# Routing tokens to experts in another order, and the first attention's keys ahead of its second queries

## The reference: what is computed

```python
x = x + L0_xattn(layernorm(x), ctx, mask, Wq, Wk, Wv, Wo)   # 16 query heads, 8 kv heads
x = x + L0_ffn(layernorm(x), ...)                           # width 1536, weights rounded to fp8
x = x + L1_xattn(layernorm(x), ctx, ..., gq, gk)            # q and k RMS-normalised
x = x + L1_ffn(layernorm(x), gate_w, gate_up, down)         # 16 experts, best 2 of each token

# routing, in L1_ffn
p = sigmoid(x @ gate_w.T)
p = p / sum(p)
w, idx = top_k(p, 2)
w = w / sum(w)
```

## Time and profile of the kernel before

| | us |
|---|---|
| median of 3 runs (lowest to highest) | 2182.91 (2182.68 to 2184.34) |
| the profiled execution, device time | 2181.82 |
| its span in the trace | 2180.0 |
| busy in the span: PE / DVE / ACT / POOL | 2073.1 / 1565.5 / 1258.0 / 504.5 |
| mean granted TensorE clock | 0.984 of 2.4 GHz |

### The profile page before, as it was taken

The page is one execution under the profiler, slowest core; times in us unless marked ns, Lnnn a source line. Parts: engine busy times, 40 slices in busy tenths (PEclk is TensorE's granted clock), DMA queues, the critical chain, the costliest instruction groups (busy, mean ns, idle before and its releaser), DMA issues. The chain is left out here.

```text
span 2180.0 us, 33659 instructions
## 1 busy us (share of the span) xinstructions
PE 2073.1 (95%) x11642; PEld 1788.1 (82%) x11642; DVE 1565.5 (72%) x3690; ACT 1258.0 (58%) x3249; POOL 504.5 (23%) x622
## 2 busy tenths in 40 slices
PE   7999999999999999999999999999999999599992
PEld 6888888988888778887888888888888887378882
DVE  6777687677779984434777777777777778767775
ACT  5555454445455534324776676777666666567771
POOL 2001011001000002223233333323332322145441
PEclk9999999999999999999999999999999999799996
DMA  7231222122221220002111111111221111288876
GB/s 256 78 124 67 73 81 90 59 90 69 85 74 39 80 71 1 1 0 78 49 62 65 58 49 59 49 58 49 71 72 53 49 40 39 87 279 291 292 270 258
DMA packets 78536, 202.51 MB, mean 93 GB/s; under 512 B 8688, under 2 KB 38408, under 8 KB 66208
## 3 DMA queue, kind: packets, MB, share of 16 engines
q1 hardware_dynamic: 68672, 179.37, 23.5%
q0 software_dynamic: 7520, 16.80, 2.3%
q10 hardware_dynamic: 2176, 4.19, 0.5%
HBM read 179.09 MB, written 29.10 MB: 95 GB/s over the span
## 5 line engine op out<-in xcount | busy, mean ns | idle before, releaser
L1319 DVE TENSOR_TENSOR l_pT_lo<-bank,l_pT_hi 128x512 fp32r<-128x512 f32 x256 | 175.4, 685 | 70.6 <-ACT l_pT_hi L1123 70.6
L1117 ACT ACTIVATE l_probs<-l_scored,l_nbias 128x256 f32<-128x256 f32 x256 | 128.6, 505 | 165.8 <-DVE l_nbias L1392 165.8
L755 PE MATMUL bank<-l_wkv_hi,l_ctxT 128*128 128x512 f32 (+1 forms) x768 | 221.1, 359 | 1.5 <-PEq L92 0.6
L755 PE MATMUL bank<-xnT_hi,l_wq_hi 128*128 128x512 f32 x512 | 209.0, 408 | 1.4 <-DVEq L1665 0.7
L755 PE MATMUL bank<-l_wo_hi,l_oT_hi 128*128 128x512 f32 x512 | 209.1, 408 | 0.7 <-DVE l_oT_lo L1319 0.7
L755 PE MATMUL bank<-l_wo_hi,l_oT_lo 128*128 128x512 f32 x512 | 200.6, 392 | 0.0
L755 PE MATMUL bank<-xnT_hi,l_wq_lo 128*128 128x512 f32 x512 | 200.2, 391 | 0.0
L755 PE MATMUL bank<-xnT_lo,l_wq_hi 128*128 128x512 f32 x512 | 199.9, 390 | 0.0
L755 PE MATMUL bank<-l_wo_lo,l_oT_hi 128*128 128x512 f32 x512 | 199.8, 390 | 0.0
L1407 DVE TENSOR_SCALAR l_probs<-l_probs,l_rden 128x256 f32<-128x256 f32 x512 | 187.8, 409 | 9.0
L1123 ACT CAST l_pT_hi<-bank 128x512 fp32r<-128x512 f32 x256 | 150.7, 589 | 62.4 <-PE bank L854 58.4
(11 more groups left out here) (299 smaller groups left out, 5736.5 us busy)
## 6 DMA issues: line engine op xcount, KB each, us to landing
l_ctxT<-ctx_split SPq DMA_DIRECT2D x63, 1024.0 KB, 4.8
moe_raw_gu<-in_L_ffn_gate_up_proj SPq DMA_DIRECT2D x31, 1024.0 KB, 6.4
moe_raw_dn<-in_L_ffn_down_proj SPq DMA_DIRECT2D x31, 512.0 KB, 5.5
l_raw_a<-in_L_xattn_Wq SPq DMA_DIRECT2D x16, 512.0 KB, 5.8
l_raw_a<-in_L_xattn_Wo SPq DMA_DIRECT2D x16, 512.0 KB, 5.8
x_sb<-in_x SPq DMA_DIRECT2D x4, 1024.0 KB, 8.2
l_v_next<-l_kn SPq DMA_DIRECT2D x16, 256.0 KB, 2.0
l_v_lo<-l_v_next SPq DMA_DIRECT2D x16, 256.0 KB, 2.6
```

What stands on the lines that cost most here:

```text
L755: mm = nc.tensor.matmul(out, a[x], b[y], start=(i == 0), stop=(i == n - 1))
L1117: ins = nc.scalar.activation(probs[u % 2][:, t, :], src, ACT.Exp, bias=nbias[:, i:i + 1], scale=scale, accum_out=rsum[:, i:i + 1])
L1319: nc.vector.tensor_tensor(pair[1], src, pair[0].bitcast(F32), ALU.subtract).then_inc(done, 1)
```

## The change

It moves and removes instructions at the two places.

First attention: on DVE the mask bias goes ahead of both query splits, and the key split ahead of the second query split; the first `biases` goes ahead of the turned rows' low parts. On ACT the key copy goes ahead of the normalisations (now three rows together) and of the second query copy. On PE the first scores go ahead of all four row transposes.

Routing: ACT normalises tiles 8 to 11 and takes the sigmoids of groups 0 and 1 in the second attention's block, with the table load at `gate_high`; PE transposes group 0's sigmoids there. In the experts block ACT, POOL and DVE normalise tiles 14, 15 and 12 to 13; there are two `probT` tiles, five turn banks, one copy out of PSUM for two groups. The division by the sum moves from `best_two` (3 instructions in each call) to behind the list of rows (4 instructions). The two multiply and sum steps ahead of the halves become one pair of double width.

```diff
@@ first attention @@
             pe.sem_inc(y_made, TG)
-            if AHEAD:
-                turn_rows(0, 1)
             scores(0, 0, 0)
             if AHEAD:
-                turn_rows(2, 3)
+                turn_rows(0, 1, 2, 3)
...
+                copy_q(*PROLOGUE, 0)
+                copy_k(*PROLOGUE, 0)
+                normalise(0, 1, 2)
+                copy_q(*PROLOGUE, 1)
             if AHEAD:
-                normalise(2, 3)
+                normalise(3)
                 act.wait_ge(k.ctx_stored, 16 * NG)
                 turned_high(0, 1)
             exponentials(0, 0, 0)
...
                 first_moments()
+                dve.wait_ge(const_in, 16)
+                nc.vector.tensor_scalar(mask_bias[:, :], mask_u8[:, :], -MASKED, MASKED, ALU.mult, ALU.add).then_inc(dve_chain, 1)
+                dve.wait_ge(dve_chain, 1)
...
                 split_q(*PROLOGUE, 0)
-                split_q(*PROLOGUE, 1)
-                dve.wait_ge(const_in, 16)
-                nc.vector.tensor_scalar(mask_bias[:, :], mask_u8[:, :], -MASKED, MASKED, ALU.mult, ALU.add).then_inc(dve_chain, 1)
-                dve.wait_ge(dve_chain, 1)
             dve.sem_inc(o_split, 1)
             for h in range(nkv):
                 split_k(*PROLOGUE, h)
+            split_q(*PROLOGUE, 1)
...
+            biases(0, 0, 0)
             if AHEAD:
                 turned_low(0, 1)
-            biases(0, 0, 0)
@@ end of the second attention, PE then ACT @@
                     following.logits(pe, g)
+                following.turn_probs(pe, 0)
...
                 following.gate_high(act)
+                act.wait_ge(ln_factors, LATE // TG + 2)
+                following.normalise(act, LATE)
+                following.sigmoids(act, 0)
+                for t in range(LATE + 1, LATE + TG):
+                    following.normalise(act, t)
+                following.sigmoids(act, 1)
@@ experts block, POOL, PE, ACT @@
+            gp.tensor_scalar(xn[:, POOL_TILE, :], k.x_sb[:, POOL_TILE, :], rstd[:, POOL_TILE:POOL_TILE + 1], shift[:, POOL_TILE:POOL_TILE + 1],
+                             ALU.mult, ALU.add).then_inc(pool_normed, 1)
...
-            for t in range(LATE, LATE + TG):
-                turn(t)
-            turn_probs(0)
-            for t in range(LATE + TG, NT):
-                turn(t)
-            turn_probs(1)
+            start.turn_probs(pe, 1)
+            for t in range(LATE, NT):
+                turn(t)
...
             for t in range(LATE, LATE + TG):
                 turned_high(t)
-            nc.scalar.activation(warm[:, 0:1], k.ident[:, 0:1], ACT.Sigmoid)
-            sigmoids(0)
-            turned_high(LATE + TG)
             copy_probs(0)
-            sigmoids(1)
-            turned_high(LATE + TG + 1)
-            copy_probs(1)
-            for t in range(LATE + TG + 2, NT):
+            for t in range(LATE + TG, NT):
                 turned_high(t)
             for g in (2, 3):
-                sigmoids(g)
-                copy_probs(g)
+                start.sigmoids(act, g)
+            copy_probs(1)
@@ experts block, DVE @@
-                chain(v.tensor_reduce(ms[:, at], prob[:, at, :], AX.X, ALU.add))
-                chain(v.reciprocal(ms[:, at], ms[:, at]))
-                chain(v.tensor_tensor(prob[:, at, :], prob[:, at, :], each(ms[:, at], E), ALU.mult))
...
+            chain(v.tensor_tensor(hsel[:, :, :, :].rearrange("p c t e -> p c (t e)"), pick[:, :, :, :].rearrange("p c t e -> p c (t e)"),
+                                  per(place[:, :, :].rearrange("p t e -> p (t e)"), 2), ALU.mult))
+            chain(v.tensor_reduce(half[:, :, :], hsel[:, :, :, :], AX.X, ALU.add))
             for c in range(2):
-                chain(v.tensor_tensor(hsel[:, c, :, :], pick[:, c, :, :], place[:, :, :], ALU.mult))
-                chain(v.tensor_reduce(half[:, c, :], hsel[:, c, :, :], AX.X, ALU.add))
...
+            chain(v.tensor_reduce(ms[:, :], prob[:, :, :], AX.X, ALU.add))
+            chain(v.reciprocal(ms[:, :], ms[:, :]))
+            chain(v.tensor_tensor(m1[:, :], m1[:, :], ms[:, :], ALU.mult))
+            chain(v.tensor_tensor(m2[:, :], m2[:, :], ms[:, :], ALU.mult))
```

More of the change, by code:

```diff
@@ L2151, in logits, with normalise, sigmoids, turn_probs @@
         mm.then_inc(a.logits_made, 1)
+    def normalise(act, t):
+        nc.scalar.activation(a.xn[:, t, :], k.x_sb[:, t, :], ACT.Identity, bias=k.ln_shift[:, t:t + 1],
+                             scale=k.ln_rstd[:, t:t + 1]).then_inc(a.early_normed, 1)
+    def sigmoids(act, g):
+        act.wait_ge(a.logits_made, g + 1)
+        if g >= 2:
+            act.wait_ge(a.probs_turned, g - 1)
+        nc.scalar.activation(a.probT[g % 2][:, :], a.b_logits[g % 2][0:E, :], ACT.Sigmoid).then_inc(a.sigmoids_made, 1)
+    def turn_probs(pe, g):
+        pe.wait_ge(a.sigmoids_made, g + 1)
+        for t in range(TG):
+            at = TG * g + t
+            mm = nc.tensor.transpose(a.b_probs[:, E * at:E * (at + 1)], a.probT[g % 2][:, P * t:P * (t + 1)], k.ident[0:E, 0:E])
+        mm.then_inc(a.probs_turned, 1)
     a.turn_gate, a.gate_high, a.gate_low, a.logits = turn_gate, gate_high, gate_low, logits
+    a.normalise, a.sigmoids, a.turn_probs = normalise, sigmoids, turn_probs
     a.sync = lambda sp: sp.dma_start(a.gw[:, :], gate_w).then_inc(a.gw_in, 16)
@@ L2172, in moe_stage @@
     BY_PAIR, BY_HALF = (1.5 * 2.0 ** 23 * n for n in (2 * P, P))
-    DVE_TILES = tuple(range(LATE + TG, NT))
-    ACT_TILES = [t for t in range(LATE, NT) if t not in DVE_TILES]
+    DVE_TILES, ACT_TILE, POOL_TILE = (LATE + TG, LATE + TG + 1), LATE + TG + 2, LATE + TG + 3
     y_rows = nc.dram_tensor("moe_y_rows", (2 * T, D), F32, kind="Internal").ap()
@@ L2195, in moe_stage @@
         assert nc.sbuf_base == w_at + 4 * (4 * GU + 4 * DN)
-        xn = at_place("xn", w_at, [P, NT, D], F32)
+        xn = start.xn
+        assert w_at == start.xn_at
         dn_at = w_at + 4 * 4 * GU
@@ L2420, in _ @@
             for g in (2, 3):
-                turn_probs(g)
+                start.turn_probs(pe, g)
             pe.wait_ge(consts_made, 14)
@@ L2503, in _ @@
         def _(act):
-            def normalise(t):
-                nc.scalar.activation(xn[:, t, :], k.x_sb[:, t, :], ACT.Identity, bias=shift[:, t:t + 1], scale=rstd[:, t:t + 1]).then_inc(act_normed, 1)
             def turned_high(t):
                 act.wait_ge(turned, t - LATE + 1)
-                nc.scalar.copy(k.xnT_hi[:, :, P * t:P * (t + 1)], b_turn[t % len(b_turn)][:, :].rearrange("p (k t) -> p k t", k=KD)).then_inc(turned_hi, 1)
-            def sigmoids(g):
-                act.wait_ge(logits_made, g + 1)
-                due(act, probs_turned, g)
-                nc.scalar.activation(probT[:, :], b_logits[g % 2][0:E, :], ACT.Sigmoid).then_inc(sigmoids_made, 1)
@@ L2516, in copy_probs @@
-            def copy_probs(g):
-                act.wait_ge(probs_turned, g + 1)
-                nc.scalar.copy(prob[:, of_group(g), :].rearrange("p t e -> p (t e)"), b_probs[:, 0:TG * E]).then_inc(probs_copied, 1)
-            for t in ACT_TILES:
-                normalise(t)
+                nc.scalar.copy(k.xnT_hi[:, :, P * t:P * (t + 1)], turn_bank(t)[:, :].rearrange("p (k t) -> p k t", k=KD)).then_inc(turned_hi, 1)
+            def copy_probs(i):
+                at = slice(*PARTS[i])
+                act.wait_ge(probs_turned, 2 * (i + 1))
+                nc.scalar.copy(prob[:, at, :].rearrange("p t e -> p (t e)"), b_probs[:, E * at.start:E * at.stop]).then_inc(probs_copied, 1)
@@ L2522, in _ @@
+            nc.scalar.activation(xn[:, ACT_TILE, :], k.x_sb[:, ACT_TILE, :], ACT.Identity, bias=shift[:, ACT_TILE:ACT_TILE + 1],
+                                 scale=rstd[:, ACT_TILE:ACT_TILE + 1]).then_inc(start.early_normed, 1)
             for t in range(LATE, LATE + TG):
                 turned_high(t)
-            nc.scalar.activation(warm[:, 0:1], k.ident[:, 0:1], ACT.Sigmoid)
-            sigmoids(0)
-            turned_high(LATE + TG)
             copy_probs(0)
-            sigmoids(1)
```

84 lines of the change are left out of this document (42 added, 42 removed).

## The result

| | before | after |
|---|---|---|
| median, us (lowest to highest) | 2183.19 (2182.68 to 2184.34, 4 runs) | 2169.29 (2169.04 to 2169.92, 4 runs) |
| the profiled execution, device time | 2181.82 | 2169.92 |
| its span | 2180.0 | 2167.8 |

I had forecast 2173.3 us, in a range of 2170.3 to 2177.3. The sign and the largest term were right; the size was not. The times in this document are of one state of the core; a single execution of before_filler ran in another (2995.85 us at a mean granted clock of 0.652) and is left out of its ratio.

A forecast was written before the change was run, and what follows sets the result against it. TensorE's waits at the first attention and in routing's chain were taken as what can be gained: 2.0 - 0.2 + 7.65 + 0.05 + 0.4 - 0.3 = 9.6, so 2182.9 - 9.6 = 2173.3 us, range 2170.3 to 2177.3.

The forecast's parts named there:

- the step on the four new instructions: Behind the list: some 1.2 us of DVE work delays the expert weights' low parts, covered by over 2 us in hand.
- First attention: Start of the kernel: earlier key copy and mask work bring scores to 38.8 and turned probabilities to 46.05, gain 2.0.
- the hold of POOL: First attention: DVE's mask work over POOL's power costs POOL all of DVE's 1.2 us, so factors come at 37.85.
- The unstretched walk: First attention without POOL losing time to the mask work: turning at 45.0, gain 3.0 in place of 2.0.
- rival (a): Mask work doesn't stretch POOL's power, and TensorE keeps 2.4 GHz through the ranking: gains 3.0 and 0.5, 2171.8 us; chance 0.22.
- Block start: Second attention's tail: with ACT last, the experts block begins at 1859.85 in place of 1859.65, cost 0.2.
- Routing: Experts block: second logits from 1864.4, not 1870.50, and the choice ends at 1875.3, not 1882.95, gain 7.65.
- (b): Routing: TensorE's clock falls during the turns, 2.5 to 4 us lost, 2176.5 us; chance 0.15.
- (c): Routing is moved but not shortened, gathered rows wait for something not moved: 2180.5 us; chance 0.03.
- (d): Clock falls before the turns and returns only behind the filling matmuls: 11.5 lost against 9.6, 2184.8 us; chance 0.02.
- Merged step: Ahead of the halves: two multiply and sum steps of double width take 1.45 us where four took 1.83, gain 0.4.
- Filling matmuls: Ahead of the expert loop: nothing can be gained, and a later return of the clock loses 0.3.

The follow-up runs named there:

- before_filler: The kernel before with four more DVE instructions, writing a tile nobody reads, ahead of the first expert weights' low parts; 2180.72 us against 2182.42, ratio 0.9992.
- before_load_waits: The kernel before with SP's second gate and up load waiting for the second gather's landing; 2180.97 us against 2182.07, ratio 0.9996.
- after_again: The changed kernel run once more, unchanged, beside the kernel before on the same chip; 2169.14 us, ratio 0.9939.
- divide_first: The changed kernel with the division by the probabilities' sum also ahead of the choice again, three instructions for each half of the tokens; 2170.32 us.
- keep16: The changed kernel with 16 filling matmuls ahead of the experts in place of 24; 2168.39 us.
- tail_undone: The changed kernel with ACT's normalising of tiles 8 to 11, the first two sigmoids and TensorE's first turn back in the experts block; 2173.7 us.

## Why the prediction was wrong

**What failed: the step on the four new instructions.** It said that they stand behind the list, delay the first expert weights' low parts, that over 2 us are in hand, and so cost nothing. The cover was there, and the cost was nothing. But I asked only who needs the low parts, and not what the low parts release. They free the buffer that SP's next load waits for; SP's issue moved from 0.9 us ahead of the third gather to 0.7 behind it, and the gathers landed early. First to fourth turning took 1.63 us less, forecast 0. before_filler and before_load_waits show it. The loop from the first filling matmul to the end, which I had put at 277 us as before, took 276.2 (277.4 before). Rows 7 had the filling matmuls and the first turning, but no gather, no load, and not the second to fourth turning: the prediction carried the loop over as a block of 277 us, though its opening isn't steady.

**First attention: the mechanism was right, its size wrong.** Scores at 38.8: 38.76. The term was the hold of POOL: from rows 4, where a DVE instruction of 0.54 us lay inside a power that took 0.49 more, I read that POOL loses all of DVE's time, and took 1.2 us. That step failed: the row's power ended 0.05 us behind DVE's instruction, and in the four traces of the table where the power loses time it is its end that is held. In rows 4 another of DVE's one-input instructions, 1043.52 to 1044.06, lies over the power's start, so that place alone could be read in more than one way. My own estimate of the landing, 34.4, would then have given DVE's end at 35.7, ahead of the power's own end at 35.97, and a loss of 0. Measured were 0.77 (after, where the mask had landed by 33.70 and POOL's small first instruction was held), 0 (after_again) and at most 0.42. The unstretched walk gave turning at 45.0, and it came at 44.95 in after_again and at 44.95 to 45.29 in six of the eight traces with the early mask: this part of rival (a) fits better than my forecast. Its other part, the full clock through the ranking, didn't come (0.54 in 1870 to 1896). The rule of the Trainium skill ("SBUF — State Buffer", section "SBUF: two separate sides") that I had weighed there, that the second to come is blocked for a whole instruction, fits none of the table's rows: the second was DVE, and it took its 1.23 us in each.

**Block start: 0 for 0.2.** ACT's last sigmoids end at 1856.87 and POOL's factors at 1856.70; the distance from the first logits to the block start is 6.63 us in both kernels, so by these two traces ACT's tail had just room; what sets the distance isn't shown. The sum also held this cost twice: the walk through the experts block starts at 1859.95, so its end of the choice at 1875.3, and with it the 7.65, already had the later start in it. Without that slip the forecast would have been 2173.1.

**Routing: right.** 4.17 us to the second logits (forecast 4.5), 15.15 to the end of the choice (15.4), in all 8.13 for 7.7. Clock at 1.00 through the turns, as the forecast needed; rivals (b), (c) and (d) are out. Of the missing 0.4, some 0.2 are the start counted twice; the rest is that turns took 3.97 us and no more, and DVE's low parts ran without gaps. **Merged step: right**, 0.37 for 0.4; **division: right**, 0.91 for 0.9 by divide_first.

**Filling matmuls: -0.68 for -0.3.** The granted clock came back 4.3 us after the first filling matmul (2.4 before), and the matmuls took 7.74 us. In the other traces with 24 of them it came back after 1.7 to 4.7 us, and they took 6.51 to 7.91. The prediction said that nothing can be gained at this place; in keep16 the fourth turning came 1.35 us sooner after the first filling matmul than in after. Before, the rows landed just as the filling ended; in the changed kernel they land sooner, and the filling is a loss.

**The range.** I gave unknown costs, all on one side: what might be lost at the filling matmuls, what POOL might lose. For an earlier opening of the loop there was no term and no rival, so the range ended at 2170.3. With 1.6 for the opening and rival (a)'s first attention (3.0), the same sum would have given some 2170.7 us. The rest (about 1.4) is the distance of single executions from their medians, the start counted twice and small gains in three places; it isn't taken apart further.

## What to carry to other kernels

When an instruction is put in "where there is room", follow what the delayed instructions release, not only who consumes their results: a freed buffer starts a transfer, and the order of transfers decides what lands in time. A large load that isn't needed soon should be issued behind the small gathers that are; one wait on the loading queue gave the shorter opening here, without any detour over an engine. And where filling work meets data that lands at the same time, a change that brings the data forward makes the filling the bound: cut it then.

## What the runs showed of the hardware that I had not expected

- Gathers of POOL's queue beside a 1024 KB load of SP's (for the second of them 512 KB more): landing after 6.0 and 7.7 us, where it is 3.5 and 4.2 when the load is issued after the first of the two has landed.
- A gather instruction of POOL took 2.08 us beside DVE's two low parts, 1.27 us when it started 0.86 us ahead of them, 1.37 us when it started 0.73 us into the first of them, 1.00 us alone.
- POOL's 1.64 us power beside a one-input DVE instruction of 1.23 us: DVE's isn't slower, and the power ends no earlier than 0.04 us behind DVE's instruction. It lost 0, 0, 0.04, 0.06, 0.18 and 0.42 us in six traces, by when DVE began.
- Two executions of the same code differ by up to 1.5 us in the second attention: from the first exponentials there (1032.50 in before) to the copy of the turned gate (1847.41) it took 814.9 to 816.4 us in the fifteen traces. The granted clock of 1040 to 1050 us was 1.00 in some and 0.83 in others, but doesn't go with it (815.6 at 1.00 in after_again, 815.1 at 0.83 in tail_undone). The cause stays open.
